# A four-layer graph network on one core: bias rows and own halves inside the matmuls, small turns between wide products, two chains reordered

## The reference

```python
# layer 0: three rounds of max pooling over the edges
h1 = relu(h @ Wp1.T + bp1);             p1 = pool_max(h1)
x  = relu(concat[h, p1] @ Wm1.T + bm1); p2 = pool_max(x)
y2 = relu(concat[x, p2] @ Wm2.T + bm2); x = layernorm(y2 + x)*g2 + b2; p3 = pool_max(x)
y3 = relu(concat[x, p3] @ Wm3.T + bm3); out = layernorm(y3 + x)*g3 + b3
# layer 1: relu(h @ w_in + b_in), then 3 times edge softmax attention:
#          h = relu(agg @ wp + bp + h)
# layer 2: two relation MLPs per node, m = relu(relu(h@W.T+b)@W.T+b), segment sum,
#          LSTM-like gates i, g, o, then W1, W2 (relu), W3
# layer 3: h @ weight[r] for 8 relations, gathered by edge type, segment mean,
#          plus h @ sl_w.T + sl_b
```

## Time and profile before

| | us |
|---|---|
| median of 3 runs (lowest, highest) | 5206.68 (5201.36, 5224.11) |
| the profiled execution, its own time | 5208.02 |
| its span in the trace | 5206.2 |
| busy: PE, PEld, DVE, ACT, POOL | 2274.8, 1539.3, 2898.2, 1032.0, 3253.7 |
| granted TensorE clock, mean over the span | 0.735 of full speed |

### The profile page before, as it was taken

One profiled execution on the slowest core, in us unless ns is written; L12 is line 12 of the kernel. 1 busy time (PEld: TensorE's weight loads), 2 busy tenths in 40 slices (PEclk: granted clock), 3 DMA queues, 4 the chain that ended last, 5 costly groups with the idle time before them and its releaser, 6 DMA issues.

```text
span 5206.2 us, 55711 instructions
## 1 busy us (share of the span) xinstructions
PE 2274.8 (44%) x12272; PEld 1539.3 (30%) x12272; DVE 2898.2 (56%) x8718; ACT 1032.0 (20%) x2805; POOL 3253.7 (62%) x3347
## 2 busy tenths in 40 slices
PE   3130240013200677778777787777810007872100
PEld 2020220002100455556555555555710003431000
DVE  7754343345443778887788878887433331114433
ACT  1000100001000343335333343333400004430000
POOL 4767677765777377773777637774067771017776
PEclk7555655556555899999999999999955558985555
DMA  5656566655666333332333323332166662136665
GB/s 172 199 167 218 187 208 205 208 179 182 208 205 208 127 98 104 106 106 76 96 106 104 94 82 106 104 106 82 40 207 208 208 205 77 74 120 207 206 206 191
DMA packets 273900, 780.32 MB, mean 150 GB/s; under 512 B 64562, under 2 KB 95795, under 8 KB 269747
## 3 DMA queue, kind: packets, MB, share of 16 engines
q0 software_dynamic: 159984, 437.08, 30.2%
q1 hardware_dynamic: 113602, 339.68, 16.7%
HBM read 459.57 MB, written 316.93 MB: 149 GB/s over the span
## 4 chain that ended last, share of the span: by engine, by line
PE 31%; POOL 26%; issue 14%; DVE 14%; DMA 13%; ACT 1%; DVEq 1%; SPq 0%; POOLq 0%; ACTq 0%
POOL HC L468 25%; PE PS L1199 9%; DMA HC<-table,run_max 7%; PE PS L1191 6%; DVE W L1797 4%; PE PS L922 4%; PE PS L1124 3%; PE PS L1180 2%; DMA HC<-table_typ,run_typ 2%; DMA HC<-table_rel,run_rel 2%; DVE HC L1603 2%; DVE HC L1861 2%; DVE work L1805 1%; PE PS L916 1%; DVE score L1805 1%
## 5 line engine op out<-in xcount | busy, mean ns | idle before, releaser
L1603 DVE SCALAR_TENSOR_TENSOR HC<-HC,run_rst 128x256 f32<-128x256 f32 x1950 | 946.3, 485 | 1395.2 <-DMA HC<-table,run_max 736.4
L468 POOL DMA_INDIRECT HC<-table,run_max x1173 | 1150.3, 981 | 468.1 <-issue 318.9
L446 POOL DMA_INDIRECT HC<-table,idx_src x648 | 637.7, 984 | 436.8 <-DMA table<-B 215.1
L1037 PE MATMUL PS<-ident,HC 128*128 128x128 f32 x10 | 3.4, 445 | 1604.2 <-DVE HC L1603 1604.2
L446 POOL DMA_INDIRECT X<-table,idx_src x600 | 581.1, 968 | 184.4 <-issue 136.5
L1861 DVE SCALAR_TENSOR_TENSOR HC<-HC,fcol,PS 128x257 f32 x1248 | 592.5, 475 | 158.4 <-PE PS L1199 140.0
L468 POOL DMA_INDIRECT HC<-table_typ,run_typ x391 | 377.3, 965 | 442.0 <-DMA table_typ<-HC 323.2
L1191 PE MATMUL PS<-AM,work 128*128 x3744 | 634.8, 282 | 0.0
L468 POOL DMA_INDIRECT HC<-table_rel,run_rel x391 | 377.3, 965 | 323.4 <-DMA table_rel<-AM 204.6
L1037 PEld LDWEIGHTS PS<-ident,HC 128*128 128x128 f32 x10 | 1.4, 203 | 1607.1 <-DVE HC L1603 1099.6
L1191 PEld LDWEIGHTS PS<-AM,work 128*128 128x128 bf16 x3744 | 373.4, 100 | 173.0 <-issue 7.2
(11 more groups left out here) (244 smaller groups left out, 3841.3 us busy)
## 6 DMA issues: line engine op xcount, KB each, us to landing
prefix<-HC SPq DMA_DIRECT2D x485, 512.0 KB, 3.1
table_typ<-HC SPq DMA_DIRECT2D x19, 1024.0 KB, 3.8
HC<-table,run_max POOLq DMA_INDIRECT x1173, 2.8
HC<-table,idx_src POOLq DMA_INDIRECT x648, 2.8
table<-AM SPq DMA_DIRECT2D x15, 640.0 KB
table<-B SPq DMA_DIRECT2D x15, 640.0 KB
X<-table,idx_src POOLq DMA_INDIRECT x600, 2.8
table_rel<-AM SPq DMA_DIRECT2D x10, 640.0 KB, 4.8
```

What stands on the lines that cost most here:

```text
L446: pool.indirect_dma_start(held(t)[:, 0:D], None, table, bass.IndirectOffsetOnAxis(ap=idx_src[:, t:t + 1], axis=0)).then_inc(landed[t % AHE ...
L468: pool.indirect_dma_start(run_slot(k), None, src, bass.IndirectOffsetOnAxis(ap=run_idx[s[1]][:, j:j + 1], axis=0)).then_inc(landed[k], 16)
L1603: V.scalar_tensor_tensor(run_slot(k), run_slot((j - 1) % SLOTS), run_rst[:, j:j + 1], run_slot(k), fade, join).then_inc(pooled, 1)
```

## The change

Seven edits, taken together:

1. `dense` can continue a sum in PSUM (`begun=True`). `bias_row` begins one: a bfloat16 product of ones with `bias_parts`, whose rows 0, 32 and 64 hold three bfloat16 parts of the bias row. DVE makes them once (`split_row`, seven small operations) for `bp1` and for `b_in`.
2. embed: the bias is added by that product; DVE's L1538 goes, and ACT applies relu straight from PSUM. DVE waits for two bias rows instead of `stored`; SP loads the second of them earlier.
3. ends of the three max rounds: a product `ident x H[b]` in float32 begins each sum; DVE's `add_ends` goes; `residual` reads PSUM (in round 1 ACT does).
4. ends of round 3: `b_in` is added by `bias_row`; DVE's `add_in` goes, and ACT reads PSUM.
5. last finish: the lags of turn, first, second and relation add grow by one; PE's order becomes turn, dense, turn, second, first; DVE's relation add, now of block i-10, stands first in its step.
6. ends of the relation runs: the turned ends of q+3 stand one by one between the wide products of batch 0, the W3 products of q+1 between those of batch 2, the turned nodes of q+1 between those of batch 3; ACT's copies follow. On ACT the four square roots stand between gate activations 3 and 4 instead of ahead of all six, and the tanh of the cell ahead of batch 3.
7. A semaphore count of its own (`out`) for `mm_out`, which is no longer raised once per product.

```diff
@@ embed, SP's loads
                     load_row("bp1", 0)
+                    load_row("bm1", 1)
...
-                    load_row("bm1", 1)
@@ ACT, embed
-                        if 0 <= i - 5 < BLOCKS:
-                            b = i - 5
-                            act.wait_ge(mm_out, m0 + b + 1)
-                            nc.scalar.activation(A[:, b, :], H[:, b, :], ACT.Relu).then_inc(rows_made, 1)
+                        if 0 <= i - 4 < BLOCKS:
+                            b = i - 4
+                            act.wait_ge(mm_done, m0 + b + 1)
+                            nc.scalar.activation(A[:, b, :], PS[:, b % 2, 0:D], ACT.Relu).then_inc(rows_made, 1)
@@ ACT, ends of the relation runs
                         for k in range(4):
-                            for b, part_ in parts[k * quarter:(k + 1) * quarter]:
-                                widen(b, part_)
-                            if k < 2 and q + 1 < groups:
+                            for j in range(4):
+                                if j < quarter:
+                                    widen(*parts[k * quarter + j])
+                                if k == 0 and j < len(ends):
+                                    take_ends(ends[j])
+                                if k == 3 and j < len(after):
+                                    take_nodes(after[j])
+                            if k < 2 and after:
                                 chain(q + 1, k)
                             if k == 2:
-                                if q + 1 < groups:
-                                    for b in GATE_GROUPS[q + 1]:
-                                        root(n, b)
                                 if q + 2 < groups:
-                                    for m in range(6):
+                                    for m in range(4):
                                         gate_act(q + 2, m)
-                        if q + 2 < groups:
-                            cell(q + 2)
-                        if q + 3 < groups:
-                            for b in GATE_GROUPS[q + 3]:
-                                take_ends(b)
-                        if q + 1 < groups:
-                            for b in GATE_GROUPS[q + 1]:
-                                take_nodes(b)
+                                for b in after:
+                                    root(n, b)
+                                if q + 2 < groups:
+                                    for m in range(4, 6):
+                                        gate_act(q + 2, m)
+                                    cell(q + 2)
@@ PE, helpers and embed
+            def bias_row(bank):
+                nc.tensor.matmul(PS[:, bank, 0:D], ones_parts[:], bias_parts[:], start=True, stop=False)
...
+                            if b >= 2:
+                                pe.wait_ge(rows_made, r0 + b - 1)
+                            bias_row(b % 2)
                             pe.wait_ge(spread, t0 + b + 1)
-                            if b >= 2:
-                                pe.wait_ge(mm_out, m0 + b - 1)
                             dense(b % 2, [B_cols[:, c, cols(b)] for c in range(K2)],
-                                  [wview["Wp1"][:, c, :] for c in range(K2)]).then_inc(mm_done, 1)
+                                  [wview["Wp1"][:, c, :] for c in range(K2)], begun=True).then_inc(mm_done, 1)
@@ PE, ends of the max rounds
                                 b = i - 1
+                                if s[2] > 1:
+                                    pe.wait_ge(mm_out, o0 + BLOCKS + max(0, b - 1))
+                                elif b >= 2:
+                                    pe.wait_ge(rows_made, r0 + b - 1)
+                                else:
+                                    pe.wait_ge(mm_out, o0 + BLOCKS)
+                                nc.tensor.matmul(PS[:, (BLOCKS + b) % 2, 0:D], ident[:], H[:, b, :], start=True, stop=False)
                                 pe.wait_ge(spread, t0 + b + 1)
-                                pe.wait_ge(mm_out, m0 + BLOCKS + b - 1)
                                 dense((BLOCKS + b) % 2, [stage_out[:, b % TRS, c * P:(c + 1) * P] for c in range(K2)],
-                                      [wide_w[:, K2 + c, :] for c in range(K2)]).then_inc(mm_done, 1)
+                                      [wide_w[:, K2 + c, :] for c in range(K2)], begun=True).then_inc(mm_done, 1)
...
+                                bias_row(2 + b % 2)
                                 pe.wait_ge(spread2, u0 + BLOCKS + b + 1)
@@ PE, ends of the relation runs
                             for k in range(4):
-                                for b, part_ in parts[k * quarter:(k + 1) * quarter]:
-                                    widen(b, part_)
-                                if k < 2 and q + 1 < groups:
+                                for j in range(4):
+                                    if j < quarter:
+                                        widen(*parts[k * quarter + j])
+                                    if k == 0 and j < len(ends):
+                                        turn_ends(ends[j])
+                                    if k == 2 and j < len(after):
+                                        last_dense(q + 1, after[j])
+                                    if k == 3 and j < len(after):
+                                        turn_nodes(after[j])
+                                if k < 2 and after:
                                     chain(q + 1, k)
...
+                                if k == 2 and q + 2 < groups:
+                                    for x in range(6):
+                                        gate_mm(q + 2, x)
@@ PE, last finish (second's body and first's body unchanged)
-                        if last_layer and 0 <= i - 8 < BLOCKS:
-                            b = i - 8
+                        if last_layer and 0 <= i - 5 < BLOCKS:
+                            b = i - 5
+                            ...
+                            turn(6 + b % 2, rel_nodes[:, b % 3, :]).then_inc(turned2, 1)
+                        if last_layer and 0 <= i - 9 < BLOCKS:
+                            b = i - 9
...
-                        if last_layer and 0 <= i - 6 < BLOCKS:
-                            b = i - 6
+                        if last_layer and 0 <= i - 7 < BLOCKS:
+                            b = i - 7
@@ DVE
+            def split_row(k, at):
+                link(V.tensor_copy(bias_parts[0:1, :], brow[0:1, k, :]))
+                high = work[:, at:at + D // 2].bitcast(BF16)
+                rest = work[:, at + D // 2:at + D // 2 + D]
+                link(V.tensor_copy(high, brow[:, k, :]))
+                link(V.tensor_tensor(rest, brow[:, k, :], high, ALU.subtract))
+                link(V.tensor_copy(bias_parts[32:33, :], rest[32:33, :]))
+                link(V.tensor_copy(high, rest))
+                link(V.tensor_tensor(rest, rest, high, ALU.subtract))
+                V.tensor_copy(bias_parts[64:65, :], rest[64:65, :]).then_inc(parts_made, 1)
@@ DVE, embed
-                    dve.wait_ge(stored, 16)
+                    bias_rows_in(dve, 2)
+                    split_row(0, TRS * D)
...
-                            V.tensor_tensor(H[:, b, :], PS[:, b % 2, 0:D], brow[:, 0, :], ALU.add).then_inc(mm_out, 1)
@@ DVE, ends of the max rounds
-                        def add_ends(b):
-                            dve.wait_ge(mm_done, m0 + BLOCKS + b + 1)
-                            dve.wait_ge(mm_out, m0 + max(BLOCKS, b + 1))
-                            V.tensor_tensor(H[:, b, :], PS[:, (BLOCKS + b) % 2, 0:D], H[:, b, :], ALU.add).then_inc(mm_out, 1)
                         def residual(b):
-                            dve.wait_ge(mm_out, m0 + BLOCKS + b + 1)
-                            summed[b] = mark(V.scalar_tensor_tensor(H[:, b, :], H[:, b, :], 0.0, A[:, b, :], ALU.max, ALU.add))
+                            dve.wait_ge(mm_done, m0 + BLOCKS + b + 1)
+                            V.scalar_tensor_tensor(H[:, b, :], PS[:, (BLOCKS + b) % 2, 0:D], 0.0, A[:, b, :],
+                                                   ALU.max, ALU.add).then_inc(mm_out, 1)
...
-                        def add_in(b):
-                            dve.wait_ge(in_done, b + 1)
-                            V.tensor_tensor(H[:, b, :], PS[:, 2 + b % 2, 0:D], brow[:, 1, :], ALU.add).then_inc(in_out, 1)
@@ DVE, last finish: the relation add, the same three lines, first in the step
+                        if last_layer and 0 <= i - 10 < BLOCKS:
+                            b = i - 10
...
-                        if last_layer and 0 <= i - 9 < BLOCKS:
-                            b = i - 9
```

More of the change, by code:

```diff
@@ L83, in made @@
     each = {"embed": {"turned": 1, "mm": 1, "centred": 1, "bn": 1, "rows": 1},
-            "project": {"turned": 1, "mm": 1},
-            "finish": {"turned": 1, "mm": 1, "rows": 1}}
+            "project": {"turned": 1, "mm": 1, "out": 1},
```

(42 more changed lines are left out.)

107 lines of the change are left out of this document (42 added, 65 removed).

## The result

The changed kernel took 5133.35 us (median of 4 runs, 5131.49 to 5136.45) against 5210.65 for the kernel before beside it (4 runs, 5201.36 to 5224.11): a ratio of 0.985, 95% interval 0.9827 to 0.9874. Forecast were 5135. Measured once more (the last pair of the experiments), with five runs, it took 5121.62 against 5208.0, a ratio of 0.983 (0.9818 to 0.9846); one of the nine runs of the kernel before there took 5473.12 at a lower granted clock (0.627) and is left out of the ratio.

A forecast was written before the change was run, and what follows sets the result against it. No engine bounds the whole kernel (PE 31% of the chain); each changed stage has its own bound. The terms -6 + 8 - 4 - 9 - 22 - 40 = -73 take 5208.0 to 5135 us, 8-in-10 range 5115 to 5163.

The forecast's parts named there:

- Embed: Embed stage: DVE starts 6.5 us earlier, PE becomes the pace at 1.20 per block; -6 us, range -8 to -2.
- Ends of round 1: First max round's ends: identity product makes PE the bound, 1.52 per block against POOL's 1.24; +8 us, bounds 0 to +12.
- Ends of round 2: Second max round's ends: DVE's period falls from 1.98 to 1.79 without the add; -4 us, range -8 to +1.
- Ends of round 3: Third max round's ends: PE takes over from DVE, period 3.08 to 2.72; -9 us, range -14 to +3.
- Last finish: Last finish: PE's wait for DVE's relation add goes, block 6.32 to 4.80; -22 us, range -26 to -10.
- Relation ends: Ends of the relation runs: small products between wide ones, group 54.8 to 45; -40 us, bounds -45 to -20.
- the list of what was won: Relation group's 11 us between PE's work: W3 products 2.6, turned ends 3.2, turned nodes 2.8, wide products 1.3 to 1.7, rest gates.
- ACT did not become the bound: Rival, relation runs' ends: ACT's chain late by 4 to 5 us per group, 20 us back, total 5155; chance 0.12.
- Load and drain: Rival, relation runs' ends: each ACT table switch holds ACT a second 1.28, 13 us in all, 5148; chance 0.03.
- The finish kept no wait: Rival, last finish: PE still meets DVE once per block, period above 6, total change -51, 5157; chance 0.08.
- The granted clock in the ends: Rival, max rounds' ends: clock granted at 0.5 throughout, +121 in place of -5, total 5260; chance 0.02.
- The identity products were not hidden in gaps: Rival, max rounds' ends: identity products lie in gaps and cost less, round 1 +2, total 5125; chance 0.07.

The follow-up runs named there:

- the last pair of the experiments: On a fourth chip, changed kernel (5121.62 us, ratio to before 0.9832) beside the changed kernel with edit 3 undone in round 1 alone (5115.71, 0.9823).

## Why the prediction was right

**Embed, forecast -6, measured -7.2.** DVE's wait ended at 10.7 where 10.5 was put, the split ran from 10.67 to 13.15, 2.5 where 2.6 was put, and the first statistics began at 13.19. The period behind it was 1.19 where 1.20 was put, against 1.25.

```profile
10.67 0.28 DVE L1533 CAST bias_parts<-brow 1x256 bf16<-1x256 f32 x1 [9.30 <-DMA brow<-bias_rows]
...
13.19 0.43 DVE L1326 BATCH_NORM_STATS2 stat<-X 128x6 f32<-128x256 f32 x1
```

**Ends of round 1, +8, measured +8.2.** The product's 0.43 and PE as the bound were both right, and both were doubled and undone: +0.43, -0.43. That 25 x 0.43 = 10.8 did not become the stage's price has the reason that the text gave: before, PE at 1.08 kept catching up with POOL's gathers and waited 0.38 for the last rows to land (its turn at 632.78), so POOL's 1.24 and not PE's 1.08 was the pace to compare with.

**Ends of round 2, -4, measured -4.7.** The period of 1.79 came out exactly, from the remark that the add stood where `aggregate`'s result was awaited; a plain subtraction of 0.31 would have said 1.67.

**Ends of round 3, -9, measured -10.6** (-12.2 against the unchanged code in four other executions, 94.1 in the mean where the profile of before had 92.4). The period of 2.72 came out as 2.71. The text gave it to both edits alike; by the experiment b_in's bias row gives 0.33 of the 0.37 when it comes first, and the own half 0.04 behind it. The other order was not run.

**Last finish, -22, measured -24.2** from its first dense product to the gather, and -22.9 for the whole stretch against unchanged code in two other executions (1982.1). The reason was half right. The wait was named rightly, DVE's add behind three others, but the prediction said that the new lags took it away, "each thing that PE waits for was begun one PE step earlier". DVE's place, which it named beside them, is enough alone. The 2.3 that it took off for the deeper pipeline is not there either: with the new lags the stage took 135.1, without them 134.7.

**Relation ends, -40, measured -41.3 and -45.2 in two profiles, -41.9 for edit 6 alone.** The period was 44.3 where 45 was put: the charge of 1.1 for ACT's new order was 0.28 of wait and some 0.2 behind it. That charge, 4.4 in all, is why four intervals from one group's W3 products to the next's fell by 40.0 (215.5 to 175.5) and not by 37. The total of the first profile, -41.3, doesn't show this, because the first group lost to a lower clock what the others won. The stage in two parts, from its first gather to the first wide product of the second group and from there to its end, in the kernel before, in the changed one, and in the changed one's second profile:

```profile
4306.84:4371.84 65.00, 49.15 (x146) 25.38 (x147) 13.20 (x31) 30.89 (x56) 24.52 (x25) 0.87 0.21 67
4371.84:4661.84 290.00, 256.05 (x623) 115.04 (x622) 40.12 (x109) 113.86 (x196) 0.00 (x0) 0.95 0.22 88
4273.02:4342.24 69.22, 53.59 (x146) 27.78 (x147) 13.23 (x31) 30.40 (x56) 24.52 (x25) 0.80 0.19 60
4342.24:4586.68 244.44, 238.89 (x623) 111.30 (x622) 40.34 (x109) 108.92 (x196) 0.00 (x1) 1.00 0.26 105
4269.78:4334.12 64.34, 48.45 (x146) 25.18 (x147) 13.23 (x31) 30.36 (x56) 24.70 (x25) 0.87 0.21 66
```

The first part, put at +1, was 4.2 longer at a granted clock of 0.80 and 0.7 shorter at 0.87, the clock of before; with edit 6 alone it was 2.2 longer at 0.83. The rest, put at -41, was -45.6, and -44.5 in the second profile. So two errors cancelled in the -41.3, and with the clock granted as before the same kernel won 45.2, just past the stated bound of 45. That part of the agreement is luck.

The step that fell is the list of what was won. It counted the W3 products' 2.6 as a gain of its own; alone it was 0.3. The parts are not terms of a sum: the turns, the W3 products, the place of the roots and the clock hang on one another, and the total came out right because it was made from PE's work (43.9 a group) and not from the list.

**The rivals.** ACT did not become the bound (0.28 at its place). Load and drain did not stack (1.29 and 1.30 to the next activation). The finish kept no wait. The granted clock in the ends was 0.91, 0.89 and 0.96, not low. The identity products were not hidden in gaps in rounds 1 and 3.

**The sum.** The stages came to -82.4 against -73, and the unchanged stretches to +10.9 in that execution, which brought the total within 2 us of the forecast: luck of some 9 us. In the second profile the stages came to -84.4, the unchanged stretches to +2.8, and the medians were 86 apart; 5135 lies 13 above the time there. Part of the +10.9 is in POOL's gathers: the 1167 short intervals between them in the three max runs added to 1500.1 us in the profile of before, 1509.6 in that of after, and 1504.0 in that of edit 6 alone, which shares these runs' code with before. In the changed kernel's second profile they added to 1504.4. So it differs between executions of one code, and no cost of the change is shown in it.

## What to carry to other kernels

Sum the bounding engine's work over a steady period and compare with the period: what lies between is what an order can win, and it is a safer forecast than the list of single waits, of which each may come back at the next rendezvous. Moving an addition from DVE into a product pays only in a stage where DVE is the bound; take each stage by its own period (here 0.43 lost, 0.18 won, and 0.04 won behind an edit that had already relieved DVE). Before a pipeline is made deeper, try moving the one late instruction in its own engine's list.

## What was not expected

The same kernel took 5208 us on two chips and 6012 and 6025 on two others. Part of it stands in single long stalls in the first blocks of a stage. ACT's rows from the ends of round 1 on the third chip (edit 3 undone in round 1):

```profile
646.45 0.39 ACT L654 ACTIVATE work<-PS 128x256 f32<-128x256 f32 x1 [13.48 <-remote]
646.74 0.41 ACT L662 ACTIVATE AM<-HC 128x256 f32<-128x256 f32 x1
663.25 0.38 ACT L654 ACTIVATE work<-PS 128x256 f32<-128x256 f32 x1 [16.11 <-remote]
```

PE had turned the rows of both at 634.03 and before, and no event of this core released ACT; a few blocks behind these two the period was 1.08 as elsewhere. But the stalls are the smaller part. The same kernel was profiled there and on the fourth chip, with spans of 5912.2 and 5112.7. Of the 800 us between them 478 lie in attention (2434.7 against 1956.9 from round 3's end to the relation run, at a granted clock of 0.86 against 0.98, with no single stall of this size), 235 in the five runs, 71 in the ends of the max rounds and 17 in the relation ends. What the chips differ in stays open. The ratio of the changed code to the kernel before stayed between 0.982 and 0.988 on all, for the versions that keep edits 2, 5 and 6 (but for the one with the identity product twice, 0.9925), but on these chips a difference of 6 us cannot be read from totals.
